# Routing products in shared turns of a PSUM bank, and a Gelu call ahead of its wait, in a two-layer attention and expert kernel

## The chip, the cores and the metric

The kernel runs on one core of one Trainium2 chip. The metric is the device time of one execution in microseconds (us). TensorE is called PE below, VectorE DVE, ScalarE ACT, GpSimd POOL, and SyncE, which here only issues DMAs, SP.

## The reference, cut to what matters

The input is 32 items of 256 tokens, 128 wide. Two layers of attention, each followed by the same expert layer, are added to the running value x:

```python
x = x + attention_a(layernorm(x))     # 16 heads of 8, biases, two masked scores
x = x + ffn(layernorm(x))
x = x + attention_b(layernorm(x))     # 16 heads of 8, no biases
x = x + ffn(layernorm(x))

def ffn(x):                            # per item
    pooled = x.mean(axis=1)
    gate = softmax(pooled @ gate_w.T)              # 8 experts
    top_w, top_i = top_k(gate, 2)
    top_w = top_w / (top_w.sum(-1, keepdims=True) + 1e-08)
    h = gelu(einsum('bsd,bkcd->bksc', x, down_w[top_i]) + down_b[top_i])
    h = h * top_w
    return einsum('bksc,bkdc->bsd', h, up_w[top_i]) + (top_w * up_b[top_i]).sum(1)
```

So each item must be through its attention before its two experts are known, and the choice of experts is a short chain of very small operations: a product with gate_w, top 2 of 8, a softmax, and then the weights and biases of the chosen experts.

## The kernel before, in words

**Turns and steps.** There are 64 turns: turn t is item t of layer 1 for t below 32, item t-32 of layer 2 above. A written-out software pipeline of steps n = -6 to 70 runs all of them; each step has eight sub-steps p = 0 to 7, one for each pair of heads, and each engine's program is a function `step(engine, n, p)` called in that order. In one step the engines work on several turns: the layer norm of turn n+5, projections of q and k of turn n+4 (L890), v of turn n+3 (L918), the scores whose row maximum is sought of turn n+2 (`max_side`, L786, read by DVE's reduction L597), the transposed maxima of turn n+1 (L878), the scores that are exponentiated, of turn n (`exp_side`, L800, read by ACT's L669), and their products with v (`weigh`, L771); the end of the attention of turn n-1 (L902, L617, L929, L736 or L738, L954), the addition to x of turn n-2 (L587), and the second norm of turn n-3 (L941, L746, which also gives the pooled value).

**PSUM.** Three pairs of banks form a ring for scores, exponentials and expert products; `uses` (L288 and after) lists in which order they take it, and `fill_pair` waits for the reader of three uses before. One bank, `values_bank`, is for `weigh`. One bank, `m_bank`, is the side bank: all other products take it in turns. Before each turn PE calls `fill_m` (L153), which waits until the reader of the turn before is through.

**Bursts.** The expert layer is done for groups of four turns, group g in step BURSTS[g] (L223). In a burst PE does `down` (L812) at p = 4, ACT does four Gelu calls (L705) at the end of p = 3, PE does `up` (L827 and L835) at p = 5, and DVE adds to x (L632). Exp and Gelu lie in different tables of ACT, and a table load stands ahead of the first Gelu and of the next Exp. POOL copies the chosen experts' weights ahead of the burst (`prepare`, L420, at p = 3: one turn a step in the four steps before the burst for turns below 40, then two a step); the last eight turns' up weights are made by DVE at p = 4 (L648).

**Batches.** The experts are chosen for batches of 8, later 4 turns (L221). `batch_at(n, after)` (L239) says which batch has its moment in step n. Before the change the moments of a batch (first turn f, r rows) are:

- step f+r+3: at p = 4 PE's `logits` (L848) takes a turn of the side bank, DVE's `best_of` (L544 to L550, five linked operations) reads it at p = 4, ACT's exponential (L753) is at p = 6;
- step f+r+4: DVE's `weights_of` (L560 to L564) at p = 0, ahead of the addition L587, and `spread` (L572 to L576) at p = 2; PE's `mixes` (L854, L857) takes a turn of the side bank at p = 4, between L902 and L918, and ACT copies its results (L712, L713) at p = 3; SP sends the indices (L389) to where POOL can load them;
- step f+r+5: PE's `biases` (L864, L865) takes a turn at p = 4, ACT copies (L720, L721), POOL splits the bias in three (`split_biases`, L442) at p = 7.

DVE's operations on a batch are linked: each waits for the semaphore of the one before (`link`, L520).

## Time and profile before

| what | value |
|---|---|
| time, median of 3 runs | 1024.27 us (1018.36 to 1024.57) |
| the profiled execution's own time | 1024.45 us |
| its span, in which all rows below lie | 1022.6 us |
| first step with work of all kinds (n = 0) begins | 52.51 us |
| step 62 begins | 963.11 us |

The profiled execution took 1.85 us more than its span, and 0.2 us more than the median of the runs.

Steps are told apart in the trace by L412, POOL's first operation of p = 0, of which there is one in each step: the start of step n is taken as the start of the L412 for turn n+1. A window from one to the next is one step.

### The profile page before, as it was taken

The numbers are of one execution on the slowest core, as the hardware profiler recorded it, in microseconds if no ns is written. First come the engines' busy times: TensorE is split into PE (matmuls) and PEld (weight loads), VectorE is DVE, ScalarE is ACT, GpSimd is POOL, SyncE is SP. The second block draws the span as 40 slices with busy tenths as digits, with TensorE's granted clock in tenths as the row PEclk, the third lists the DMA queues.
The fourth block names the chain that finished last, engine by engine and source line by source line (L and its number), as shares of the span: only waits on it lengthen the run. The fifth ranks groups of instructions, "written<-read, shape, count | busy, mean of one in ns | idle before, by whom it ended". The sixth has DMA issues, their size and how long they took to land.

```text
span 1022.6 us, 27845 instructions
## 1 busy us (share of the span) xinstructions
PE 928.4 (91%) x10286; PEld 515.9 (50%) x10286; DVE 787.7 (77%) x1394; ACT 767.8 (75%) x1280; POOL 666.7 (65%) x1280
## 2 busy tenths in 40 slices
PE   2589999989999899989999999998999899998985
PEld 1245555545554555545555455555555455555444
DVE  1778888878878788787878878786887868877624
ACT  2168888868887788877887778876888778787863
POOL 8455666648767767575767667676675758773532
PEclk9889999989999999999999999998999999999987
DMA  6576455444434445343454435444354535445001
GB/s 186 152 225 196 142 139 174 134 118 137 146 113 138 130 109 148 114 146 87 136 146 129 121 105 153 117 139 122 100 149 135 150 85 162 124 117 151 12 22 42
DMA packets 144695, 131.68 MB, mean 129 GB/s; under 512 B 9616, under 2 KB 127536, under 8 KB 144432
## 3 DMA queue, kind: packets, MB, share of 16 engines
q1 hardware_dynamic: 143456, 128.49, 43.7%
q8 instruction: 83, 1.36, 0.6%
q10 hardware_dynamic: 1104, 1.41, 0.5%
q14 instruction: 52, 0.43, 0.1%
HBM read 73.76 MB, written 55.57 MB: 126 GB/s over the span
## 4 chain that ended last, share of the span: by engine, by line
PE 71%; ACT 9%; DVE 8%; issue 7%; DMA 2%; POOL 2%; ACTq 1%; SPq 0%; DVEq 0%; POOLq 0%
PE values_bank L771 22%; PE ring L786 12%; PE ring L800 11%; PE m_bank L890 6%; DVE nmax L597 6%; PE m_bank L918 4%; PE m_bank L954 3%; PE m_bank L941 3%; PE m_bank L902 3%; PE m_bank L929 2%; ACT probs L669 2%; ACT hT L705 2%; DMA k_stack<-scratch 2%; PE ring L835 1%; ACT qk L689 1%
## 5 line engine op out<-in xcount | busy, mean ns | idle before, releaser
L597 DVE TENSOR_REDUCE nmax<-ring 128x4 f32<-128x1024 f32 x512 | 605.7, 1220 | 127.1 <-PE ring L786 126.4
L669 ACT ACTIVATE probs<-ring 128x1024 f32<-128x1024 f32 x512 | 517.8, 1026 | 48.1 <-PE ring L800 43.6
L771 PE MATMUL values_bank<-probs,values 128*32 128x256 f32 x4096 | 277.5, 389 | 1.3 <-ACT probs L669 1.2
L786 PE MATMUL ring<-k_stack,q_stack 64*128 64x256 bf16 x2048 | 202.5, 278 | 24.3 <-DMA k_stack<-scratch 18.7
L488 POOL TENSOR_SCALAR xy<-x,mv,rstd 128x128 f32<-128x128 f32 x256 | 200.7, 794 | 7.9
L800 PE MATMUL ring<-q_stack,k_stack 64*128 64x256 bf16 x2048 | 190.8, 276 | 0.7 <-DVE nmax L597 0.2
L412 POOL TENSOR_SCALAR mparts<-nmax 128x32 bf16<-128x32 f32 x64 | 13.9, 217 | 226.4 <-DVE nmax L597 226.4
L771 PEld LDWEIGHTS values_bank<-probs,values 128*32 128x32 f32 x4096 | 107.6, 110 | 92.6 <-issue 39.5
L786 PEld LDWEIGHTS ring<-k_stack,q_stack 64*128 64x128 bf16 x2048 | 70.1, 95 | 136.7 <-issue 61.0
L800 PEld LDWEIGHTS ring<-q_stack,k_stack 64*128 64x128 bf16 x2048 | 79.0, 95 | 84.6 <-issue 48.0
L504 POOL TENSOR_TENSOR rest<-qk,parts 128x512 f32<-128x512 f32 x64 | 74.0, 1157 | 5.4
L510 POOL TENSOR_TENSOR parts<-rest,parts 128x512 bf16<-128x512 f32 x64 | 74.0, 1156 | 5.4
L481 POOL TENSOR_TENSOR rstd<-varp,minus_half 128x4 f32<-128x4 f32 (+1 forms) x72 | 69.4, 964 | 6.0
L730 ACT COPY values<-m_bank 128x128 f32<-128x128 f32 x128 | 29.0, 280 | 57.1 <-PE m_bank L918 57.1
L528 DVE BATCH_NORM_STATS2 raw<-x 128x6 f32<-128x128 f32 x256 | 60.9, 280 | 11.1 <-DMA x<-in_x 11.1
L587 DVE TENSOR_TENSOR x<-x,m_bank 128x256 f32<-128x256 f32 x64 | 27.0, 422 | 46.8 <-PE m_bank L954 46.5
L941 PE MATMUL m_bank<-ident,xy 128*128 128x128 f32 x256 | 45.6, 297 | 13.0 <-ACT wb L192 9.0
L501 POOL TENSOR_SCALAR parts<-qk 128x512 bf16<-128x512 f32 x64 | 39.5, 618 | 19.6 <-ACT qk L690 18.6
L743 ACT COPY xnT<-m_bank 128x256 f32<-128x256 f32 x64 | 23.8, 372 | 37.1 <-PE m_bank L941 36.9
L680 ACT COPY oT<-values_bank 128x512 f32<-128x512 f32 x64 | 37.4, 585 | 18.2 <-PE values_bank L771 18.2
L902 PE MATMUL m_bank<-ident,oT 128*128 128x128 f32 x256 | 41.9, 286 | 2.7 <-ACT oT L680 0.8
L507 POOL TENSOR_SCALAR parts<-rest 128x512 bf16<-128x512 f32 x64 | 39.5, 618 | 5.9
(100 smaller groups left out, 1083.3 us busy)
## 6 DMA issues: line engine op xcount, KB each, us to landing
q_stack<-scratch SPq DMA_DIRECT2D x128, 256.0 KB
k_stack<-scratch SPq DMA_DIRECT2D x128, 256.0 KB
scratch<-parts SPq DMA_DIRECT2D x128, 192.0 KB, 2.1
scratch<-parts SPq DMA_DIRECT2D x128, 128.0 KB, 2.1
scratch<-parts SPq DMA_DIRECT2D x128, 64.0 KB, 2.4
out<-x SPq DMA_DIRECT2D x16, 256.0 KB, 2.7
x<-in_x SPq DMA_DIRECT2D x3, 768.0 KB, 6.6
q_stack<-maxT SPq DMA_DIRECT2D x128, 12.0 KB
```

The lines of the kernel that those rows point to most:

```text
L481: nc.gpsimd.tensor_tensor(rstd[i][:, both, :], varp[i][:, both, :], minus_half[:, both, :], ALU.pow).then_inc(rstd_done, 1)
L488: last = nc.gpsimd.tensor_scalar(xy[i][:, m, t, :], x[:, (turn % ITEMS) * TILES + t, :], mv[i][:, m, t, 0:1], rstd[i][:, m, t:t + 1], ALU. ...
L504: nc.gpsimd.tensor_tensor(rest[i][:, :, :], qk32[i][:, :, :], parts[i][:, 0], ALU.subtract).then_inc(rest_done, 1)
L510: nc.gpsimd.tensor_tensor(parts[i][:, 2], rest[i][:, :, :], parts[i][:, 1], ALU.subtract).then_inc(parts_ready, 1)
L597: nc.vector.tensor_reduce(dst, src, axis=AX.X, op=ALU.max, negate=True).then_inc(max_done, 1)
L669: nc.scalar.activation(probs[g % 2][:, c:c + 2, :, :], pair_of("exps", n, p)[:, :, :].rearrange("p x (k q) -> p x k q", k=TILES), ACT.Exp) ...
L771: last = nc.tensor.matmul(values_bank[32 * c:32 * (c + 1), a * TOKENS:(a + 1) * TOKENS], values[turn % RING][:, k, PER_GROUP * g + c, :], ...
L786: last = nc.tensor.matmul(pair_of("scores", turn, p)[:, a, t * TOKENS:(t + 1) * TOKENS], q_stack[z][rows, p, t * P:(t + 1) * P], k_stack[z ...
L800: last = nc.tensor.matmul(pair_of("exps", turn, p)[:, a, k * TOKENS:(k + 1) * TOKENS], k_stack[r][rows, p, k * P:(k + 1) * P], q_stack[r][ ...
L890: last = nc.tensor.matmul(m_bank[:, a * TOKENS:(a + 1) * TOKENS], wmat, xnT[(n + 4) % 2][:, :], start=(a == 0), stop=(a == 1), skip_group_ ...
L902: last = nc.tensor.transpose(m_bank[:, at:at + P], oT[(n - 1) % 2][:, a, t * P:(t + 1) * P], ident[:, :])
L941: last = nc.tensor.transpose(m_bank[:, at:at + P], xy[(n + 5) % 2][:, m, t, :], ident[:, :])
```

## The change

- `logits` now stands at p = 7 of step f+r+2, in the side bank's columns 256 to 263, in the turn of the output projection L954 that follows it in the same turn (columns 0 to 255); the next taker of the bank waits for `best_of`'s first reading.
- `best_of` stands at p = 0 of step f+r+3, behind the addition L587 and ahead of the step's first maximum; ACT's exponential is at p = 2; `weights_of` and `spread` are at p = 5, behind the additions of a burst.
- `mixes` stands at p = 1 of step f+r+4 in columns 128 to 287, and `biases` at p = 1 of step f+r+5 in columns 128 to 383, each sharing the turn of the transposed maxima L878, which as 16-bit values take the bytes of columns 0 to 127. ACT's copies stand behind its copy of the maxima (L676), ahead of `oT` (L680). `split_biases` stays in step f+r+5.
- BURSTS is new, so that for the batches of turns 8 to 47 step f+r+3 is a burst step. Its first eight entries are two steps later. The two-a-step preparation begins at turn 32 instead of 40.
- In a burst ACT calls Gelu on one column (`spare`) ahead of its first wait; in bursts of steps 64 and above it calls Exp on one column behind the last Gelu.
- DVE's up weights for turns 56 to 63 are made at p = 7 instead of p = 4.

```diff
-        BURSTS = (17, 21, 25, 29, 33, 37, 41, 45, 49, 53, 55, 57, 59, 63, 66, 70)
+        BURSTS = (19, 23, 27, 31, 35, 39, 43, 47, 49, 51, 54, 56, 58, 62, 66, 70)
...
-                early_step = burst - (1 if turn >= LATE else GROUP - j if turn < 40 else 2 - j // 2)
+                early_step = burst - (1 if turn >= LATE else GROUP - j if turn < ITEMS else 2 - j // 2)
...
-            return next((b for b, (first, rows) in enumerate(BATCHES) if first + rows + BACK + after == n), None)
+            return next((b for b, (first, rows) in enumerate(BATCHES) if first + rows + BACK - 1 + after == n), None)
...
-                    if p == 7 and batch_at(n, 2) is not None:
-                        split_biases(batch_at(n, 2))
+                    if p == 7 and batch_at(n, 3) is not None:
+                        split_biases(batch_at(n, 3))
...
-                    link(nc.vector.tensor_scalar(logit[rows, :], m_bank[rows, 0:EXPERTS], 1.0 / TOKENS, None, ALU.mult))
+                    link(nc.vector.tensor_scalar(logit[rows, :], m_bank[rows, TOKENS:TOKENS + EXPERTS], 1.0 / TOKENS, None, ALU.mult))
...
-                    if p == 0 and batch_at(n, 1) is not None:
-                        weights_of(batch_at(n, 1))
                     if p == 0 and live(n - 2):
...
+                    if p == 0 and batch_at(n, 1) is not None:
+                        best_of(batch_at(n, 1))
...
-                    if p == 2 and batch_at(n, 1) is not None:
-                        spread(batch_at(n, 1))
...
-                    if p == 4 and batch_at(n, 0) is not None:
-                        best_of(batch_at(n, 0))
...
+                    if p == 5 and batch_at(n, 1) is not None:
+                        weights_of(batch_at(n, 1))
+                        spread(batch_at(n, 1))
...
-                    if p == 4:
+                    if p == 7:
                         for turn in PREPARED.get(n, ()):
                             if turn >= FIRST_BY_VECTOR:
...
+                    if p == 0 and batch_at(n, 2) is not None:
+
+                        b = batch_at(n, 2)
+                        act.wait_ge(mixed_done, b + 1)
+                        if before_batch(b):
+                            act.wait_ge(wu_ready, before_batch(b))
+                        nc.scalar.copy(weight[b % 2][:, :], m_bank[:, WIDTH:WIDTH + ITEMS])
+                        nc.scalar.copy(hotT[:, :, :].rearrange("p a b -> p (a b)"), m_bank[0:TOP * EXPERTS, WIDTH + ITEMS:WIDTH + 5 * ITEMS]).then_inc(weight_ready, 1)
+                    if p == 0 and batch_at(n, 3) is not None:
+
+                        b = batch_at(n, 3)
+                        act.wait_ge(biases_done, b + 1)
+                        if b > 0:
+                            act.wait_ge(split_done, SPLITS * b)
+                        nc.scalar.copy(biasd[b % 2][:, :], m_bank[:, WIDTH:WIDTH + ITEMS])
+                        nc.scalar.copy(biasu[:, :], m_bank[0:3 * ITEMS, TOKENS:TOKENS + WIDTH]).then_inc(biases_ready, 1)
...
                         group = group_at(n)
+                        nc.scalar.activation(spare[:, group:group + 1], bqs[:, :], ACT.Gelu)
                         act.wait_ge(biases_ready, batch_of(group * GROUP) + 1)
...
+                        if n >= TURNS:
+                            nc.scalar.activation(spare[:, len(BURSTS) + group:len(BURSTS) + group + 1], bqs[:, :], ACT.Exp)
...
-                    if p == 6 and batch_at(n, 0) is not None:
-
-                        b = batch_at(n, 0)
+                    if p == 2 and batch_at(n, 1) is not None:
+
+                        b = batch_at(n, 1)
...
+                    if p == 1 and batch_at(n, 2) is not None:
+                        mixes(batch_at(n, 2))
+                    if p == 1 and batch_at(n, 3) is not None:
+                        biases(batch_at(n, 3))
                     if p == 1 and live(n + 1):
-                        fill_m(pe, maxT_ready, (n + 1) + 1)
+                        if batch_at(n, 2) is None and batch_at(n, 3) is None:
+                            fill_m(pe, maxT_ready, (n + 1) + 1)
...
-                    if p == 4 and batch_at(n, 0) is not None:
-                        logits(batch_at(n, 0))
-                    if p == 4 and batch_at(n, 1) is not None:
-                        mixes(batch_at(n, 1))
-                    if p == 4 and batch_at(n, 2) is not None:
-                        biases(batch_at(n, 2))
...
+                    if p == PAIRS - 1 and batch_at(n, 0) is not None:
+                        logits(batch_at(n, 0))
                     if p == PAIRS - 1 and live(n - 1):
                         wo = projections[(n - 1) // ITEMS][3]
-                        fill_m(pe, x_ready, (n - 1) + 1)
+                        if batch_at(n, 0) is None:
+                            fill_m(pe, x_ready, (n - 1) + 1)
```

## Rows read from the trace of the kernel before

**Rows 1.** The page: busy time by engine, and shares of the chain that ended last.

```profile
PE 928.4 (91%) x10286; PEld 515.9 (50%) x10286; DVE 787.7 (77%) x1394; ACT 767.8 (75%) x1280; POOL 666.7 (65%) x1280
...
PE 71%; ACT 9%; DVE 8%; issue 7%; DMA 2%; POOL 2%; ACTq 1%; SPq 0%; DVEq 0%; POOLq 0%
```

**Rows 2.** Busy time in single steps 25, 31, 33, 35, 36, 13.

```profile
core 0: us, PE busy (x) PEld busy (x) DVE busy (x) ACT busy (x) POOL busy (x), PEclk, DMA share, GB/s
388.06:401.04 12.98, 12.88 (x153) 6.86 (x154) 11.48 (x19) 10.89 (x19) 10.10 (x20) 1.00 0.51 145
482.01:494.82 12.81, 12.78 (x153) 6.83 (x153) 11.48 (x19) 10.72 (x18) 10.11 (x20) 1.00 0.47 136
520.48:538.48 18.00, 16.78 (x181) 10.53 (x182) 12.95 (x21) 14.88 (x24) 10.10 (x19) 1.00 0.43 116
551.32:565.60 14.28, 13.00 (x155) 6.94 (x156) 12.16 (x24) 10.87 (x20) 10.10 (x19) 1.00 0.51 141
565.60:581.72 16.12, 14.77 (x158) 7.31 (x159) 13.00 (x27) 10.99 (x20) 10.16 (x19) 0.89 0.40 117
...
229.48:243.59 14.11, 13.57 (x157) 7.34 (x158) 11.57 (x19) 11.26 (x21) 11.79 (x24) 1.00 0.50 135
```

**Rows 3.** The same, summed over the three-step stretches of batches 0 to 7.

```profile
sum 392.69, PE 358.64 PEld 200.78 DVE 304.32 ACT 296.18 POOL 245.16; mean PE 44.83 PEld 25.10 DVE 38.04 ACT 37.02 POOL 30.65
```

**Rows 4.** Timeline of burst steps 33 and 63: start, us, engine, instruction, [idle before].

```profile
525.45 1.94 ACT L669 ACTIVATE probs<-ring 128x1024 f32<-128x1024 f32 x2
...
527.41 1.99 PE L812 MATMUL ring<-normT,wd 128*128 128x256 f32 x8
...
528.61 1.28 ACT L705 ACT_TABLE_LOAD   x1 [1.22 <-issue]
...
531.53 0.39 PE L827 MATMUL ring<-biasu_parts,pick 96*128 96x256 bf16 x2 [1.14 <-ACT hT L705]
...
978.70 1.28 ACT L705 ACT_TABLE_LOAD   x1 [0.42 <-issue]
```

**Rows 5.** Timeline of batch 3's steps 35 and 36, the product and linked operations.

```profile
559.50 0.14 DVE L544 TENSOR_SCALAR logit<-m_bank 8x8 f32<-8x8 f32 x1
...
559.70 0.71 PE L918 MATMUL m_bank<-wb,xnT 128*128 128x128 f32 x4 [1.25 <-DVE logit L544]
...
560.13 0.14 DVE L550 TENSOR_SCALAR nbest<-best 8x1 f32<-8x1 f32 x1
...
576.79 1.93 PE L771 MATMUL values_bank<-probs,values 128*32 128x256 f32 x16
```

**Rows 6.** Timeline of the last batch: first and last of weights_of and spread.

```profile
1007.92 0.20 DVE L560 TENSOR_SCALAR tsum<-e 4x1 f32<-4x1 f32 x1 [0.65 <-ACT e L753]
...
1009.41 0.17 DVE L576 TENSOR_TENSOR mix<-hot,wt 4x16 f32<-4x16 f32 x1
```

**Rows 7.** Timeline of the beginning of step 37.

```profile
582.30 0.42 DVE L587 TENSOR_TENSOR x<-x,m_bank 128x256 f32<-128x256 f32 x1 [0.73 <-PE m_bank L954]
...
582.70 3.49 DVE L597 TENSOR_REDUCE nmax<-ring 128x4 f32<-128x1024 f32 x3
...
584.28 0.39 PE L800 MATMUL ring<-q_stack,k_stack 64*128 64x256 bf16 x4
```

**Rows 8.** Timeline of POOL at the end of step 54, and splitting of batch 3's bias.

```profile
852.58 1.16 POOL L510 TENSOR_TENSOR parts<-rest,parts 128x512 bf16<-128x512 f32 x1
853.74 0.22 POOL L412 TENSOR_SCALAR mparts<-nmax 128x32 bf16<-128x32 f32 x1
...
593.02 0.29 POOL L448 TENSOR_SCALAR biasu_parts<-biasu 96x128 bf16<-96x128 f32 x1
...
594.64 0.42 POOL L456 TENSOR_TENSOR biasu_parts<-biasu_rest,biasu_mid 32x128 bf16<-32x128 f32 x1
```

**Rows 9.** Timeline of the end: steps 65 and 70.

```profile
998.85 2.54 DVE L648 TENSOR_SCALAR wu<-up_sb,weight 64x128 f32 x8 [2.89 <-issue]
...
1016.90 1.16 PE L835 MATMUL ring<-wu,hT 128*128 128x128 f32 x8 [0.34 <-ACT hT L705]
```

More of the change, by code:

```diff
@@ L120, in build @@
         biasd = [sb(f"biasd{i}", [P, ITEMS]) for i in range(2)]
+        spare = sb("spare", [P, 32])
         biasu = sb("biasu", [3 * ITEMS, WIDTH])
@@ L847, in logits @@
                         pe.wait_ge(consts_in, 16 * CONSTANTS)
-                    nc.tensor.matmul(m_bank[0:rows, 0:EXPERTS], pooled[:, at], gate_sb[:, :], start=True, stop=True).then_inc(logits_done, 1)
+                    nc.tensor.matmul(m_bank[0:rows, TOKENS:TOKENS + EXPERTS], pooled[:, at], gate_sb[:, :], start=True, stop=True).then_inc(logits_done, 1)
                 def mixes(b):
@@ L853, in mixes @@
                     pe.wait_ge(mixing, MIXING * (b + 1))
-                    nc.tensor.transpose(m_bank[:, 0:ITEMS], wide[:, :, :].rearrange("p a b -> p (a b)"), ident[0:ITEMS, 0:ITEMS])
+                    nc.tensor.transpose(m_bank[:, WIDTH:WIDTH + ITEMS], wide[:, :, :].rearrange("p a b -> p (a b)"), ident[0:ITEMS, 0:ITEMS])
                     for k in range(4):
                         src = (hot if k == 0 else mix)[:, :, :].rearrange("p a b -> p (a b)")
-                        last = nc.tensor.transpose(m_bank[0:TOP * EXPERTS, (k + 1) * ITEMS:(k + 2) * ITEMS], src, ident[0:ITEMS, 0:ITEMS])
+                        last = nc.tensor.transpose(m_bank[0:TOP * EXPERTS, WIDTH + (k + 1) * ITEMS:WIDTH + (k + 2) * ITEMS], src, ident[0:ITEMS, 0:ITEMS])
                     last.then_inc(mixed_done, 1)
@@ L863, in biases @@
                     pe.wait_ge(weight_ready, b + 1)
-                    nc.tensor.matmul(m_bank[:, 0:ITEMS], downb_sb[:, :], hotT[:, 0, :], start=True, stop=True)
-                    nc.tensor.matmul(m_bank[0:3 * ITEMS, WIDTH:2 * WIDTH], hotT[:, 1:4, :].rearrange("p a b -> p (a b)"), upb_sb[:, :],
+                    nc.tensor.matmul(m_bank[:, WIDTH:WIDTH + ITEMS], downb_sb[:, :], hotT[:, 0, :], start=True, stop=True)
+                    nc.tensor.matmul(m_bank[0:3 * ITEMS, TOKENS:TOKENS + WIDTH], hotT[:, 1:4, :].rearrange("p a b -> p (a b)"), upb_sb[:, :],
                                      start=True, stop=True).then_inc(biases_done, 1)
```

14 lines of the change are left out of this document (removed).

## The prediction

> **What bounds the kernel now.** I read the page's busy shares and its chain first. PE is busy 91% of the span and holds 71% of the chain that ended last; DVE, ACT and POOL are busy 77, 75 and 65% [rows 1]. So whatever makes PE idle costs time, and whatever the others do beside it costs nothing until it makes PE wait. Then I cut the run into steps. A plain step is 12.98 us in layer 1 and 12.81 in layer 2 with PE busy 12.88 and 12.78: PE is the whole step. DVE is busy 11.48 of it, ACT 10.9, POOL 10.1 [rows 2]. These give what each could take on for nothing: DVE 1.33, ACT 1.9 to 2.1, POOL 2.7 before its gaps between instructions.
>
> Everything above the plain step is what the change can touch. A burst alone makes a step 18.00, 5.19 more, of which PE works 4.00 (16.78 less 12.78) and idles 1.19. The first step of a batch is 14.28, the second 16.12, and the third 14.11 where no burst shares it, 1.47, 3.31 and 1.13 more, for 0.22, about 0.5 and 0.7 of PE's work [rows 2]. (In the second PE is busy 1.99 more at a granted clock of 0.89. Its products with v took 1.93, nearly twice the 1.07 of a plain step's, behind its waits: PE ran part of this step at 1.2 instead of 2.4 GHz [rows 2, 5].) The cause of the first is plain: `logits` has a turn of the side bank, and PE's next product waits 1.25 for DVE's reading, which stood behind DVE's long reductions [rows 5].
>
> **Gelu's table ahead of the wait.** In step 33 ACT's exponentials end at 527.39, it idles 1.22, loads the table from 528.61 (1.28) and then does four Gelu, and PE waits 1.14 for them before it may begin `up` [rows 4]. The idle time is the wait for the first two products of `down`. The new call lets the load begin at 527.4: table there at 528.7, the one-column Gelu about 0.2 more, so the first real Gelu starts at 528.9 instead of 529.9. The other two wait for the last `down` product at 529.40 and are not held by it. `up` may begin 1.0 earlier, inside the 1.14 that PE waits. So 1.0 a burst is gone; it is PE's time, as PE has work behind it. Thirteen bursts begin before step 62 in either order: 13.0. Bounds: 0.5 if the next Exp and its load become late instead, 1.19 (PE's whole idle time) at best: 6.5 to 15.5.
>
> One rule speaks against this. The Trainium skill (ScalarE: Activation LUTs, What ACT_TABLE_LOAD costs) says that a switch costs a drain of about 1.38 us beside the load of 1.283. If the idle 1.22 were that drain, the load could not come earlier and the gain would be nil. The load is 1.28 here too; but the idle time ahead of it is 1.22 in step 33 and 0.42 in step 63 [rows 4], as a wait for products would have it and a fixed drain not. By the rule the sum below would be 1002.7 instead of 989.0; it is rival 4.
>
> **The batches before.** The stretches of three steps of batches 0 to 7 sum to 392.69 [rows 3]. Without batches they would be 7 steps of 12.97, 15 of 12.82, steps 60 and 61 (where q, k and v of later turns are missing) of about 11.4 each, an estimate, and 8 bursts of 5.19: 90.8 + 192.3 + 22.8 + 41.5 = 347.4. The batches cost 45.3, 5.7 each.
>
> **The batches after.**
> - `logits`: its product is 0.22 of PE [rows 2] and has no wait of its own: the output projection L954 behind it uses the same turn, and L878 in the next step waits for DVE's first linked operation, 0.18 behind the addition it waited for anyway. 0.25.
> - `best_of`, now ahead of the step's first reduction: from 559.50 to 560.27, 0.8 us [rows 5], all five operations and gaps. DVE runs three reductions back to back from 582.70; PE's exponential-side product of p = 1 needs the first, done at 583.92, and started at 584.28 [rows 7]. So 0.36 is slack and 0.45 shows; the third reduction (3.49 for three) is tighter, and I take 0.7. Bounds 0.2 to 0.8. Behind it queue all of the step's maxima.
> - ACT's exponential of 0.3 to 0.5 between the third and fourth: 0.2, in front of Gelu.
> - `weights_of` and `spread`: from 1007.92 to 1009.58, 1.7 us [rows 6], at p = 5. Before, DVE's burst steps had 18.00 less 12.95 idle, 5 us [rows 2]; the operations fill the wait ahead of the reductions of p = 6, and PE needs these only a product with v later. 0.1 in a burst, 0.7 where there is none (batches 0, 6, 7), since a plain step leaves DVE 1.33. Bounds 0 to 1.7.
> - `mixes`: 0.5 of PE in p = 1, no wait for `o` ahead and none for ACT's copies behind, because L878 shares the turn and the copies fit into the time in which ACT waits for `weigh` before `oT`. 0.5.
> - `biases`: 0.7 in the same way.
> That is 2.45 for batches 1 to 5 and about 3.0 for 0, 6 and 7: 12.2 + 9.0 = 21.2. The gain is 45.3 less 21.2, 24.1. The least is PE's work alone, 1.45 a batch, 11.6 in all.
>
> **POOL and the queues.** In steps 52, 53 and 56, 57 POOL prepares two turns a step. A step with two preparations fills POOL wholly already: in step 54 it went from L510 (852.58 + 1.16) straight into the next step's L412 [rows 8]. Steps 53 and 57 have now no burst, and the split of the bias comes on top: 593.02 to 595.06, 2.0 [rows 8], less the 0.7 by which `biases` lengthens them. Behind it on POOL stand the split maxima, for which PE's L878 waits with nearly no slack. 1.4 twice: 2.8 lost. Bounds 0 to 5.6. The queue of SP gains nothing and loses nothing: the index DMA goes out a step ahead of its use, as before. The changed turns of the bursts let no later user of x or of the ring wait: each group is added to x before the item's second visit, seven steps ahead in the case of group 0.
>
> **The end.** From step 62 on, ACT's exponentials bind more than PE, and at the very end it is one chain. Gelu early: 0.4 in the burst of step 62 (its idle time of 0.42 [rows 4]) and 0.34 in the last, what `up` waited for Gelu [rows 9]. `mixes` out of the way of step 64's chain: about 0.4. In step 65 DVE's up weights (2.89 of register loads and waiting, 2.54 of work [rows 9]) move behind the statistics of the last turn, so these come 5 earlier; but the norm's transposes stand behind `up` in PE's queue, and `up` waits for these weights, now 0.8 later. I take 0 for it, bounds 2.5 won to 1.5 lost. Sum 1.2.
>
> **The sum.** 1024.45 - 13.0 - 24.1 + 2.8 - 1.2 = 989.0, against the profiled execution's own time; it stood 0.2 above the median, which I leave out. Check: from 52.5 to 963.1 PE cannot go below the sum of its work, and the kernel would need 910.6 - 34.3 = 876 there, still above 62 plain steps and 13 bursts of 4.0 (about 852) and the batches' own 12.
>
> **Rivals.**
> 1. The forecast, 989: chance 0.60.
> 2. All but PE's own work hides: batches cost 11.6, no loss on POOL, and the bursts as forecast. For it: ACT and DVE have 2 and 1.3 us to spare. Against: DVE's three reductions back to back. 1024.45 - 13.0 - 33.7 - 1.2 = 976.6. Chance 0.14.
> 3. DVE becomes the bound of each batch: `best_of` and `weights_of` with `spread` show in full, 0.8 + 1.7 beside 1.45 and 0.2 of ACT, 4.15 a batch, 33.2 in all; and Gelu gives only 0.5 a burst. 1024.45 - 6.5 - 12.1 + 2.8 - 1.2 = 1007.5. Chance 0.15.
> 4. The early Gelu does nothing, because what stands ahead of the table load is not the wait that it passes: 989.0 + 13.0 + 0.7 = 1002.7. For it: the trace names no releaser for that idle time, only "issue". Against: it varies. Chance 0.08. This is what the Trainium skill's drain (ScalarE: Activation LUTs, What ACT_TABLE_LOAD costs) would do.
> 5. Slower: PE's clock. The one batch step that stalls most in the kernel before has a granted clock of 0.89 for a stall of about 1.3; if the stall at the head of `best_of`'s step and what follows leaves PE at 1.2 GHz for most of the batch's three steps, 38 us of PE's work grow by up to a factor of two. At a granted clock of 0.75 that is 38.4 / 0.75 - 38.4 = 12.8 a batch on top of 2.65, for eight batches 124 against 45.3: 1024.45 - 13.0 + 78.5 + 2.8 - 1.2 = 1091. It decides from where a batch costs over 7.1 (45.3 and the net 11.4 of the other terms, by eight). Against it: 1.14 of idle in a burst left the clock at 1.00 [rows 2, 4]. Chance 0.03.
>
> **Numbers.** A measurement of this kernel tells about 1% from no change. Faster by over 1% (below 1014) holds in cases 1 to 4 but for their edges: 0.95; within 1% 0.03; slower 0.02. The range takes in rival 2 and reaches to rival 4: 976 to 1005.
>
> **What would show it.** Burst steps of about 17.0 with ACT's table load right behind the exponentials and no wait of 1.1 at L827; steps 34 (logits) at 13.1, 36 (mixes) at 13.3, 37 (biases) at 13.5, 35 (burst, `best_of`) near 18.0 with PE waiting for L597 at its start; steps 53 and 57 ending with POOL late and a PE wait for L418; steps before 10 unchanged. Wrong it would be if the load keeps its idle time ahead (rival 4), if step 35 is above 19 (rival 3), or if the granted clock falls below 0.95 in the batches' steps (rival 5).

## The result and the profile after

The changed kernel takes 991.04 us, the median of 4 runs (988.27 to 991.77), against 1024.42 (1018.36 to 1024.73) for the kernel before beside it: a ratio of 0.9692, with a 95% interval of 0.9657 to 0.9727. The forecast was 989.0 in a range of 976 to 1005. The profiled execution took 990.56 us; its span is 987.4, where the forecast less the 1.85 around the span of before was 987.15.

The page's busy shares and its chain, to be set beside [rows 1]:

```profile
PE 917.8 (93%) x10286; PEld 513.9 (52%) x10286; DVE 787.2 (80%) x1394; ACT 772.6 (78%) x1299; POOL 666.2 (67%) x1280
...
PE 67%; ACT 10%; DVE 9%; POOL 5%; issue 4%; DMA 3%; SPq 1%; POOLq 1%; ACTq 1%; DVEq 0%
```

The same products run, and yet PE is busy 10.6 us less, in a span 35.2 shorter. "Issue" fell from 7% of the chain to 4%: it is 7% again in e1 and 4% in e2 below, which differ from their base in the early Gelu call alone, so what left it is the wait ahead of Gelu's table. Next the busy time of single steps of the kernel after, cut as in [rows 2]: 34 (logits at its end), 35 (burst with `best_of`), 36 (mixes), 37 (biases), 47 (burst alone), then 53 to 57, and the whole stretch from step 0 to step 62:

```profile
core 0: us, PE busy (x) PEld busy (x) DVE busy (x) ACT busy (x) POOL busy (x), PEclk, DMA share, GB/s
514.58:527.42 12.84, 12.81 (x155) 6.83 (x155) 11.47 (x19) 10.66 (x18) 10.11 (x20) 1.00 0.49 149
527.42:545.60 18.18, 17.52 (x187) 11.01 (x188) 14.81 (x34) 15.88 (x27) 10.09 (x19) 1.00 0.36 111
545.60:558.33 12.73, 12.61 (x154) 6.65 (x155) 11.57 (x19) 10.36 (x20) 10.10 (x20) 1.00 0.42 135
558.33:571.80 13.47, 13.44 (x157) 7.34 (x158) 11.58 (x19) 11.04 (x20) 11.82 (x25) 1.00 0.53 153
697.46:714.36 16.90, 16.78 (x181) 10.53 (x182) 12.86 (x21) 14.98 (x25) 11.40 (x25) 1.00 0.39 121
787.91:802.82 14.91, 14.73 (x172) 7.99 (x171) 12.56 (x21) 12.26 (x21) 13.10 (x31) 1.00 0.64 190
802.82:821.16 18.34, 16.94 (x167) 10.31 (x167) 12.08 (x20) 13.80 (x24) 11.39 (x24) 0.91 0.34 104
821.16:837.27 16.11, 13.81 (x164) 7.49 (x164) 14.79 (x33) 11.77 (x20) 11.41 (x25) 1.00 0.41 126
837.27:854.05 16.78, 16.39 (x182) 10.15 (x177) 12.79 (x21) 14.58 (x27) 11.39 (x24) 1.00 0.45 135
854.05:868.95 14.90, 14.82 (x172) 8.08 (x172) 12.48 (x21) 12.25 (x21) 13.09 (x29) 1.00 0.38 114
...
52.79:926.28 873.49, 853.02 (x9825) 474.63 (x9826) 744.74 (x1280) 727.29 (x1206) 614.08 (x1168) 1.00 0.47 138
```

The same stretch of the kernel before:

```profile
52.51:963.11 910.60, 865.36 (x9825) 478.23 (x9826) 745.68 (x1280) 724.71 (x1193) 611.92 (x1159) 0.98 0.46 133
```

The reader is to see three things. A burst step went from 18.00 [rows 2] to 16.90, with PE busy 16.78 in both: its idle time went from 1.22 to 0.12. The batch's burst (35) costs 1.28 more than a burst alone, its second step (36) nothing, its third (37) 0.64. And the stretch to step 62 is 37.1 us shorter; 24.8 of that is idle time (45.2 before, 20.5 after) and 12.3 is PE's busy time with the granted clock at 1.00 instead of 0.98. About 2.2 of the 37.1 lie in step 0, ahead of every changed instruction: it took 14.73 before and 12.54 after, where PE waits for a DMA into `k_stack`, and between 13.2 and 15.7 in the experiments. So the part of the changed steps is 34.9, of which 24.0 is PE's idle time and 11.0 its busy time (1.3 of the 12.3 lie in step 0). In the profile of before, steps 12, 28, 36, 44, 45 and 52 have a granted clock below 1.00; in that of after step 54 alone has.

What became of the wait for Gelu's table, in the timeline of step 35 (start, duration; compare [rows 4]):

```profile
534.07 1.00 ACT L669 ACTIVATE probs<-ring 128x1024 f32<-128x1024 f32 x1
...
535.09 1.28 ACT L713 ACT_TABLE_LOAD   x1
...
536.38 0.20 ACT L713 ACTIVATE spare<-bqs 128x1 f32<-128x1 f32 x1
536.49 1.55 ACT L722 ACTIVATE hT<-ring,biasd 128x256 f32<-128x256 f32 x4
...
538.10 0.39 PE L830 MATMUL ring<-biasu_parts,pick 96*128 96x256 bf16 x2
```

The exponential ends at 535.07 and the load starts at 535.09. The first product of `up` (L830, L827 before) waits for nothing. The idle time ahead of this load is 0.02 in all thirteen bursts up to step 61; in the kernel before it was 0.93 to 1.35 there. The load for the next Exp had 0.02 to 0.56 ahead of it already before the change.

What `best_of` at the head of the step does, same timeline, some 5 us earlier:

```profile
528.77 0.11 PEld L886 LDWEIGHTS m_bank<-identb,mparts 128*128 128x128 bf16 x2 [0.21 <-DVE logit L545]
...
529.27 3.49 DVE L598 TENSOR_REDUCE nmax<-ring 128x4 f32<-128x1024 f32 x3
...
530.55 0.39 PE L803 MATMUL ring<-q_stack,k_stack 64*128 64x256 bf16 x4 [0.49 <-DVE nmax L598]
```

The transposed maxima (L886) are held by DVE's first reading for a moment only. Three reductions stand back to back as in [rows 7], but start later, and PE waits 0.49 for the first. The forecast had 0.45 for this.

### The profile page after: what moved, and what is told of

Read it like the earlier page. It is cut to its first block, busy times and chain, and to the rows that moved or that the text cites. A ratio compares the mean times of both kernels' runs of the same rounds, so it can differ in the third digit from the quotient of the medians.

```text
span 987.4 us, 27821 instructions
## 1 busy us (share of the span) xinstructions
PE 917.8 (93%) x10286; PEld 513.9 (52%) x10286; DVE 787.2 (80%) x1394; ACT 772.6 (78%) x1299; POOL 666.2 (67%) x1280
## 4 chain that ended last, share of the span: by engine, by line
PE 67%; ACT 10%; DVE 9%; POOL 5%; issue 4%; DMA 3%; SPq 1%; POOLq 1%; ACTq 1%; DVEq 0%
PE values_bank L774 21%; PE ring L789 11%; PE ring L803 10%; PE m_bank L898 6%; DVE nmax L598 5%; PE m_bank L910 4%; PE m_bank L959 3%; PE m_bank L943 3%; PE m_bank L920 3%; ACT probs L669 2%; PE m_bank L931 2%; ACT hT L722 2%; ACT L713 2%; DMA k_stack<-scratch 2%; DMA scratch<-parts 1%
## 5 line engine op out<-in xcount | busy, mean ns | idle before, releaser
L774 PE MATMUL values_bank<-probs,values 128*32 128x256 f32 x4096 | 274.9, 386 | 0.7 <-ACT probs L669 0.6
L774 PEld LDWEIGHTS values_bank<-probs,values 128*32 128x32 f32 x4096 | 107.1, 109 | 89.8 <-issue 37.2
L511 POOL TENSOR_TENSOR parts<-rest,parts 128x512 bf16<-128x512 f32 x64 | 74.1, 1158 | 5.4
L529 DVE BATCH_NORM_STATS2 raw<-x 128x6 f32<-128x128 f32 x256 | 60.9, 280 | 10.8 <-DMA x<-in_x 10.7
L586 DVE TENSOR_TENSOR x<-x,m_bank 128x256 f32<-128x256 f32 x64 | 27.0, 421 | 49.9 <-PE m_bank L959 49.9
L943 PE MATMUL m_bank<-ident,xy 128*128 128x128 f32 x256 | 44.9, 294 | 12.3 <-ACT wb L193 9.0
```

The lines of the kernel that those rows point to most:

```text
L511: nc.gpsimd.tensor_tensor(parts[i][:, 2], rest[i][:, :, :], parts[i][:, 1], ALU.subtract).then_inc(parts_ready, 1)
L529: last = nc.vector.bn_stats(raw[i][:, t, :], x[:, (turn % ITEMS) * TILES + t, :])
L774: last = nc.tensor.matmul(values_bank[32 * c:32 * (c + 1), a * TOKENS:(a + 1) * TOKENS], values[turn % RING][:, k, PER_GROUP * g + c, :], ...
L943: last = nc.tensor.transpose(m_bank[:, at:at + P], xy[(n + 5) % 2][:, m, t, :], ident[:, :])
```

## The experiments

e1 to e4 ran on one chip beside seven runs of the kernel before (median 1020.41 us), e5 to e8 on another beside one (1026.22), and e9 to e12 there beside eleven (1021.65). Step lengths are windows as above, from one profiled execution each. "Step 1 to 62" is the stretch from the start of step 1 to that of step 62; it leaves out step 0, which varies.

**1 and 2. Gelu's table.** e1 takes the early call out of the kernel after:

```diff
-                        nc.scalar.activation(spare[:, group:group + 1], bqs[:, :], ACT.Gelu)
```

> The changed kernel without the one-column Gelu call ahead of the wait. Theory: the call lets the table load overlap the wait for the first products of down, so without it a burst step without batch work (step 47) goes from 16.90 back to about 18.0, TensorE waits 1.1 at L830 again, and the kernel takes about 13 x 1.1 + 0.7 = 15 us more than 991: 1006 (ratio to the kernel before about 0.982). Rival (the drain or another stall ahead of the load is fixed, and the bursts got shorter by their new places): step 47 stays at 16.9 and the time within 2 us of 991.

e2 puts that line, and `spare`, into the kernel before and changes nothing else:

```diff
                         group = group_at(n)
+                        nc.scalar.activation(spare[:, group:group + 1], bqs[:, :], ACT.Gelu)
                         act.wait_ge(biases_ready, batch_of(group * GROUP) + 1)
```

> The kernel before with nothing but the one-column Gelu call. Theory: the gain of the call does not hang on the other edits: step 33 goes from 18.00 to 16.9, in all 1024.3 - 15 = 1009 (ratio about 0.985). Rival: in bursts that share a step with biases (steps 21, 29, 37, 45, 53, 57) the wait for the side bank, not Gelu, ends last, and half of the bursts give nothing: 1024.3 - 8 = 1016 (ratio 0.992).

Measured: e1 1005.26 us, ratio to before 0.984 (0.9791 to 0.9889); e2 1004.64, ratio 0.983 (0.9781 to 0.988). A burst alone in layer 2 is 18.00 in e1, as before, and 16.89 or 16.90 in e2, as after. The timeline of a burst in e1 (step 35):

```profile
540.01 1.00 ACT L669 ACTIVATE probs<-ring 128x1024 f32<-128x1024 f32 x1
...
542.18 1.28 ACT L721 ACT_TABLE_LOAD   x1 [1.18 <-issue]
...
545.10 0.39 PE L829 MATMUL ring<-biasu_parts,pick 96*128 96x256 bf16 x2 [1.14 <-ACT hT L721]
```

and in e2 (step 33, old place of everything else):

```profile
516.75 1.94 ACT L670 ACTIVATE probs<-ring 128x1024 f32<-128x1024 f32 x2
...
518.70 1.28 ACT L698 ACT_TABLE_LOAD   x1
...
521.71 0.39 PE L829 MATMUL ring<-biasu_parts,pick 96*128 96x256 bf16 x2
```

So the call is worth about 1.1 in most bursts in either surrounding, and rival 4 is out: without the call the load idles 1.18 behind the exponential, with it 0.01. The rival of e2's expectation is out too: a burst that shares its step with `biases` gains as much (29: 19.31 to 18.20). Less is gained where PE waited less for Gelu or still does: 0.69 in steps 55 and 59 of e2 (a wait of 0.49 before), 0.83 in step 39, where the kernel after still waits 0.30 for it. For thirteen bursts the steps of e2 give 13.8. From step 1 to step 62, e1 needs 14.2 us more than the kernel after. In e2 the same stretch is 21.1 shorter than before, 7.3 more than 13.8; experiment 12 shows what that remainder is. By the medians e2 is 15.8 under the kernel before beside it.

**3. The burst schedule.** e3 keeps everything but gives the bursts and the preparation their old steps:

```diff
-        BURSTS = (19, 23, 27, 31, 35, 39, 43, 47, 49, 51, 54, 56, 58, 62, 66, 70)
+        BURSTS = (17, 21, 25, 29, 33, 37, 41, 45, 49, 53, 55, 57, 59, 63, 66, 70)
...
-                early_step = burst - (1 if turn >= LATE else GROUP - j if turn < ITEMS else 2 - j // 2)
+                early_step = burst - (1 if turn >= LATE else GROUP - j if turn < 40 else 2 - j // 2)
```

> The changed kernel with the burst steps and the preparation rule of before, so that for batches 1 to 5 the vector operations stand in plain steps and the biases in burst steps. Theory (a plain step has 1.3 us of VectorE to spare and takes a batch's operations for about 0.6 more than a burst step does; POOL's overflow in steps 53 and 57 goes): steps 35 and 43 about 12.82 + 1.9 = 14.7, steps 53 and 57 without a POOL wait; 5 x 0.6 = 3 lost and 4 won back: 990, the same as the changed kernel. Rival (a plain step cannot take them, as step 55 of the changed kernel suggests, 3.2 above plain with its follower): steps 35 and 43 near 16, 5 x 1.9 = 9.5 lost, 4 won: 996.

Measured: 987.99 (987.71 to 988.25), ratio 0.9667 (0.9621 to 0.9713): not slower than the kernel after, whose ratio is 0.9692. The steps show why. The first line is a plain step with all of `best_of`, `weights_of` and `spread` (35), the second the third step of that batch, here a burst:

```profile
534.83:550.12 15.29, 13.79 (x163) 7.47 (x164) 13.98 (x33) 11.75 (x20) 10.10 (x19) 1.00 0.45 132
...
562.85:580.37 17.52, 17.41 (x185) 11.01 (x186) 12.96 (x21) 15.36 (x27) 11.78 (x24) 1.00 0.39 117
```

In a plain step DVE's batch operations cost 15.29 less 12.83, 2.46, between the theory's 1.9 and the rival's 3.2; in a burst 18.18 less 16.90, 1.28. So standing in bursts is worth about 1.2 a batch in layer 2 (1.0 in steps 19 and 27), and from step 1 to step 49 the kernel after is indeed 3.9 ahead of e3. From step 49 to 62 it loses 6.0: its steps 53 and 57 overflow on POOL, batches 6 and 7 still have `best_of` in plain steps (55 and 59), and a drop of the clock (below) is 1.5 of it. The new schedule as a whole is not a gain; the batches' new places are. Up to step 62, e3 differs from e2 only in these places and in the shared turns: 858.9 us from step 1 to 62 against 874.8, 15.9 less. In e2 3.3 of this lie in its steps 52 and 56, where the granted clock is 0.90 and 0.89.

Step 55 of the kernel after costs more than e3's plain step, 16.11. Its timeline:

```profile
832.82 1.16 POOL L511 TENSOR_TENSOR parts<-rest,parts 128x512 bf16<-128x512 f32 x1
...
832.98 1.08 DVE L574 COPY wide<-wt 4x128 f32<-4x128 f32 x1
...
836.03 0.39 PE L803 MATMUL ring<-q_stack,k_stack 64*128 64x256 bf16 x4 [1.76 <-DVE nmax L598]
```

The copy of `spread` takes 1.08 here, beside POOL's L511, and 0.21 in the steps of the other batches; in e3's step 35 PE's wait at this place is 0.96. So 0.8 of step 55 is the slow copy. It is there in all eight profiles with this schedule and not in e3, e8 and e10. That POOL's operation holds it is likely from the times, and was not tested.

**4. The shared turns.** e4 leaves `mixes` and `biases` at p = 1 but gives them a turn of the side bank of their own, with ACT's copies ahead of the maxima's:

```diff
-                        if batch_at(n, 2) is None and batch_at(n, 3) is None:
-                            fill_m(pe, maxT_ready, (n + 1) + 1)
+                        fill_m(pe, maxT_ready, (n + 1) + 1)
...
```

ACT's copy L676 moves behind L684 to L693.

> The changed kernel in which mixes and biases take a turn of the side bank of their own at p = 1, ahead of that of the transposed maxima (ScalarE copies their results first). Theory (sharing the turn is worth what TensorE would wait for two ScalarE copies): 0.5 to 0.9 us a step in two steps of each of eight batches, 8 x 2 x 0.7 = 11: 1002, and some clock below 1.00 in these steps. Rival (TensorE has work of values ahead that hides the copies, the place at p = 1 alone was the gain): within 3 us of 991.

Measured: 998.78 (996.07 to 1000.33), ratio 0.9767 (0.9717 to 0.9817). Step 36 is 0.68 longer than the 12.73 after, with the same work of PE:

```profile
550.52:563.93 13.41, 12.61 (x154) 6.64 (x155) 11.58 (x19) 10.44 (x20) 10.10 (x19) 1.00 0.46 140
```

and from its timeline:

```profile
552.44 0.29 PE L885 MATMUL m_bank<-identb,mparts 128*128 128x128 bf16 x2 [0.77 <-ACT hotT L679]
```

PE waits 0.77 for the copy of `hotT` before it may write the maxima. Step 37 is 14.01 instead of 13.47. Over all batches sharing is worth 8.2 us (step 1 to 62: 867.7 here, 859.45 in the second profile of the kernel after), where 11 were expected. With turns of their own at p = 1, `mixes` and `biases` still cost 0.58 and 1.18 over a plain step. In the kernel before, at p = 4, steps 36 and 37 cost 1.84 (with DVE's weights, 14.67 in e2) and 1.31 (18.20 in e2 less its burst's 16.89). The rest of the batches' gain lies in the places of DVE's and PE's operations together; they were not tested one by one.

**5. POOL's overflow.** e5 moves `split_biases` from p = 7 of the batch's third step to p = 0 of the next, behind the split maxima:

```diff
-                    if p == 7 and batch_at(n, 3) is not None:
-                        split_biases(batch_at(n, 3))
...
+                    if p == 0 and batch_at(n, 4) is not None:
+                        split_biases(batch_at(n, 4))
```

> The changed kernel with POOL's split of the bias moved from the end of a batch's third step to behind the split maxima of the next. Theory (in steps 53 and 57 the two preparations and this split overfill POOL, and PE waits for L419 in the step behind): the wait of 1.46 ahead of L886 at the start of step 54 goes, with the fall of the granted clock behind it; steps 53 and 54 together from 33.25 to about 30.4 + 0.2, 57 and 58 from 31.76 to 30.4; the time about 4 lower, 987. Rival (POOL stays too full, and the norm's transposes or the split parts are late instead): 53 and 54 together stay above 32, or steps such as 22 and 30, plain until now, grow.

Measured in one run: 988.23. Step 53 is 13.34 instead of 14.91 and step 57 13.44 instead of 14.90, so the split is what made them late, 1.5 each. But the steps behind the third steps of batches 1 to 4 are 13.18 instead of 12.95 (layer 1) or 12.81, as the rival said, and step 56 is 19.45 instead of 16.78:

```profile
789.67:803.01 13.34, 13.31 (x157) 7.21 (x157) 11.57 (x19) 10.91 (x20) 11.42 (x25) 1.00 0.65 190
...
836.00:855.45 19.45, 19.28 (x182) 11.33 (x177) 12.98 (x21) 14.62 (x27) 11.39 (x24) 0.82 0.36 115
```

In the long one PE is busy 19.28 for the work of 16.39: it ran part of it at 1.2 GHz, behind the wait of 1.76 at the end of step 55. From step 1 to 62 the gain and these losses come to within 1 us of nothing, where 4 won were expected.

**6. The order of index and store at the end.** SP issues the last index DMA ahead of the two stores of group 14 in the kernel after. The stores are in step 67 in both kernels, a step behind burst 66; the index DMA has moved with the batches from step 68 to 67, and in SP's step its block stands ahead of that of the stores. e6 exchanges the two blocks in SP's step, so that the index DMA L390 comes behind this:

```diff
+                    group = group_at(n - 1) if n <= LAST else None
+                    if group is not None and group * GROUP >= ITEMS:
+                        store(sp, group)
...
-                    group = group_at(n - 1) if n <= LAST else None
-                    if group is not None and group * GROUP >= ITEMS:
-                        store(sp, group)
```

> The changed kernel with SyncE's store of a group ahead of the index DMA in the same step. Theory (the two stores of group 14, 512 KB, run just behind the last index DMA and slow POOL's first load of a register from 0.57 to 1.59 us, and down then begins 1 us later with PE's clock still low): from the index DMA to the first L429 4.2 us instead of 5.2, and the end 1 to 2 us earlier. Rival (the slow load has another cause, as the queue state or the position of the code): still 5.2, and no gain.

Measured in one run: 987.30. The chain that ended last, near the end, in the kernel after:

```profile
969.44 1.60 DMA index<-which
971.04 0.03 issue
971.07 1.59 POOLq L324
...
976.31 3.75 PE ring L815 x8
980.07 0.43 PE ring L830 x2
```

in the kernel before:

```profile
1007.12 1.64 DMA index<-which
...
1008.78 0.57 POOLq L323
```

and in e6:

```profile
971.03 0.57 POOLq L324
...
975.22 3.75 PE ring L815 x8
```

POOL's first load of an index into a register takes 1.59 in the kernel after and 0.57 in the other two. From the index DMA to `down` (L815, L812 before) it is 5.85 before, 6.87 after, 5.86 in e6, and 6.87 to 6.90 in the eight other profiles that have the stores behind the index, e3 with its old bursts among them. So 1.0 us of the end is this order, and it came with the batches' new places and not with the new bursts. From step 62 on e6 takes 58.5, against 61.1 after and 59.5 before; what it has won beyond 1.0 lies in the pieces that vary without the change (below).

**7. `best_of` split.** e7 leaves only the first of its five operations, the one that frees the side bank, at p = 0, and puts the other four at p = 2 behind the reductions, with ACT's exponential at p = 3:

```diff
                     link(nc.vector.tensor_scalar(logit[rows, :], m_bank[rows, TOKENS:TOKENS + EXPERTS], 1.0 / TOKENS, None, ALU.mult))
+
+                def rest_of_best(b):
...
+                    if p == 2 and batch_at(n, 1) is not None:
+                        rest_of_best(batch_at(n, 1))
...
```

> The changed kernel with only best_of's first operation ahead of the step's maxima and the other four at p = 2 behind the statistics, ScalarE's exponential at p = 3. Theory (0.8 us ahead of three back-to-back reductions is what makes PE wait 0.49 for L598 at the start and again before the third): step 35 from 18.18 to about 17.6, with L803 no longer waiting 0.49; eight batches, 4 to 5 us in all. Rival (the reduction at p = 3 is as tight, so the wait only moves): step 35 stays within 0.2 of 18.18.

Measured in one run: 983.84. Step 35 is 17.73 instead of 18.18, step 59 14.18 instead of 14.73:

```profile
527.25:544.98 17.73, 17.48 (x188) 11.03 (x188) 14.68 (x34) 15.79 (x27) 10.10 (x20) 1.00 0.41 115
```

and from its timeline:

```profile
528.48 3.49 DVE L602 TENSOR_REDUCE nmax<-ring 128x4 f32<-128x1024 f32 x3
...
532.27 0.14 DVE L550 MAX8 best<-logit 8x8 f32<-8x8 f32 x1
```

The reductions start 0.6 earlier against the step's start than in the kernel after, and the four small operations fit in behind. In six of the eight batches 0.5 of `best_of`'s cost was its place ahead of the reductions; from step 1 to 62 it makes 3.0 against the second profile of the kernel after, where 4 to 5 were expected. Step 55 stayed at 16.10, with the same wait of 1.76 near its end, and step 11 at 14.9.

**8. Another schedule.** e8 puts bursts also over the third steps of the small batches:

```diff
-        BURSTS = (19, 23, 27, 31, 35, 39, 43, 47, 49, 51, 54, 56, 58, 62, 66, 70)
+        BURSTS = (19, 23, 27, 31, 35, 39, 43, 47, 51, 53, 55, 57, 59, 62, 66, 70)
```

> The changed kernel with bursts 51, 53, 55, 57, 59 in place of 49, 51, 54, 56, 58, so that biases and their split (53, 57) and best_of (55, 59) fall on burst steps, at the price of a plain step 51 under batch 5's vector operations. Theory (stated from the step lengths of the changed kernel and of e3): 53, 57 near 17.5, 55 and 59 near 18.1, 51 near 15.3; steps 49 to 61 in all 195.9, as in e3, against 199.2, so step 62 begins about 3.3 earlier than in the changed kernel. Rival (each burst has its own cost that depends on the distance to the last one): no gain.

Measured in one run: 983.07. (The expectation named 51 a plain step; it is a burst, and 49 is plain. Its 195.9 for e3 is not what e3 took, 193.1.) Steps 49 to 61 took 192.04, where the kernel after needs 199.09, 7.0 less instead of the 3.3 expected:

```profile
726.88:918.92 192.04, 186.70 (x2134) 107.23 (x2135) 161.14 (x280) 161.13 (x268) 138.62 (x303) 1.00 0.42 128
```

PE's products are as many; 1.7 less busy time and 5.3 less idle. The lower clock in step 54 of after is 1.5 of the 7.0. All of the loss that e3 does not have is gone, with the early bursts kept.

**9. The up weights at the end.** e9 returns DVE's up weights of turns 56 to 63 to their old place:

```diff
-                    if p == 7:
+                    if p == 4:
                         for turn in PREPARED.get(n, ()):
                             if turn >= FIRST_BY_VECTOR:
```

> The changed kernel with VectorE's up weights for the last eight turns back at p = 4. Theory (what the earlier statistics win, up's later start loses): PE's wait of 0.98 for L648 ahead of L830 in step 66 goes, the last statistics come 5 us later, and from the last L586 (turn 63) to the index DMA it takes 11.6 as before the change, against 11.29: 0.3 lost. Rival (the move to p = 7 costs what up waits): 10.5, 0.8 won.

Measured in one run: 990.56. The wait of 0.98 for L648 is gone and the last statistics come later, as expected. From the last addition of attention (turn 63, L586) to the index DMA it is 11.86, against 11.29 and 11.42 in the two profiles of after and 11.58 and 11.59 in those of before. The move is worth about half a microsecond at most, in one run.

**10. All that helped.** e10 has the schedule of e8, the split of e7 and the order of e6.

> What helped, together: the bursts of e8, best_of split as in e7, the store ahead of the index as in e6. Theory (the three act on different steps and add): 991 less 7.0 (of which 1.4 is a clock episode that the changed kernel's profile has and others had not), 2.8 and 1.0, about 980 to 981, ratio to the kernel before about 0.957 to 0.96; steps 35 and 43 at 17.73, 53 and 57 at 17.4, 55 and 59 at about 17.7. Rival (they share the gain, as the same waits of TensorE): 983, like the best of them alone.

Measured: 978.12 (975.49 to 979.06, 6 runs) against 1021.65 (11 runs): ratio 0.9559 (0.9527 to 0.9591). It beats both kernels. From step 1 to 62 it needs 850.5 us, the kernel after 861.0 and 859.45; against the latter it wins 9.0, e8 alone 5.5 and e7 alone 3.0, so the two add, as the theory said. Step 53, burst, biases and two preparations at once, is the case in point: 17.48 where the kernel after has 14.91 without a burst.

```profile
781.54:799.02 17.48, 17.37 (x185) 10.96 (x185) 12.96 (x21) 15.31 (x27) 13.14 (x30) 1.00 0.56 164
```

Its end is no shorter: 60.9 from step 62 on. In e8 and e10, and in e4, the last addition of attention stands 12.9 to 13.5 before the index DMA instead of 11.3; why was not looked into.

**11 and 12. Both kernels profiled again**, unchanged.

> The changed kernel once more, unchanged, for a second profile. Theory (whether a stall also costs a fall of TensorE's clock depends on when it comes, not on the step): all steps repeat within 0.03 us but for those behind a stall of about 1.5 us, where step 54 is 16.85 or 18.34; the first step differs by up to 2 us. Rival (it belongs to the step in this kernel): step 54 is 18.34 again.

> The kernel before once more, unchanged. Theory: steps 12, 28, 36, 44, 45 and 52, where its profile has a granted clock below 1.00, lie at their length with a full clock (15.3, 14.7, 14.7, 14.7, 19.3, 15.0) in some cases, and steps 20 and 56, at 14.7 there, may lie near 16.2; the other steps repeat. Rival: the same steps have the low clock again.

Measured: 988.09 and 1024.4. In the second profile of the kernel after, all steps from 1 to 61 are within 0.02 of the first, but one. Step 54 begins in both with a wait for POOL; the first profile:

```profile
804.14 0.27 PE L886 MATMUL m_bank<-identb,mparts 128*128 128x128 bf16 x2 [1.46 <-POOL mparts L419]
...
804.34 1.94 PE L774 MATMUL values_bank<-probs,values 128*32 128x256 f32 x16
```

the second:

```profile
805.25 0.27 PE L886 MATMUL m_bank<-identb,mparts 128*128 128x128 bf16 x2 [1.46 <-POOL mparts L419]
...
805.45 1.07 PE L774 MATMUL values_bank<-probs,values 128*32 128x256 f32 x16
```

and that step as a window of the second profile:

```profile
803.92:820.78 16.86, 15.42 (x167) 9.72 (x167) 11.99 (x20) 13.77 (x24) 11.40 (x24) 1.00 0.41 113
```

The same wait of 1.46 is followed by products of 1.94 in the one and 1.07 in the other, and the step takes 18.34 or 16.86. In the kernel before, the same happens to a batch's second step. Step 28 in its first and its second profile:

```profile
446.58:462.71 16.13, 14.77 (x158) 7.41 (x159) 13.01 (x27) 11.08 (x20) 10.16 (x20) 0.89 0.42 118
```

```profile
447.76:462.43 14.67, 13.30 (x158) 6.99 (x159) 13.01 (x27) 11.08 (x20) 10.18 (x19) 1.00 0.47 129
```

Six steps of before (12, 20, 21, 28, 52, 53) differ by about 1.5 between its two profiles, in both directions. Steps 36, 44 and 45 have the lower clock in both and 56 in neither, as the rival said of them. So most batches of the kernel before have one or two places where PE's clock may fall, and in six of these steps it changes from execution to execution whether it does. Its runs say the same: the eleven beside e10 go from 1018.39 us at a mean granted clock of 0.978 to 1028.75 at 0.968. This is the remainder of e2: with the early call its step 36 is 14.67 at clock 1.00, where the two profiles of before have 16.12 and 16.31, steps 28, 36, 44 and (beside the call's 1.1) 45 are 1.5 and step 12 2.9 shorter than in the first profile of before, and step 56, with the lower clock here, is 1.5 longer, in all 7.2. Whether the early call itself makes the fall less likely is open. Between steps 1 and 61 the profiles of before have six and seven steps with the clock below 1.00 and e2 has two; the eleven profiles with the batches' new places have one or none.

It is the same for the wait of 1.76 at the end of step 55: in both profiles of after the granted clock behind it stayed at 1.00, and in e1 and e5 the next step has 0.91 and 0.82 (18.98 and 19.45 us). In e4, e6 and e7, which have this wait too, it stayed. Each fall in steps 1 to 61 of all profiles follows waits of 1.2 to 1.8 in sum, more than half of them in two pieces, as 0.91 and 0.42 in step 28 of before; none follows the 1.14 of a burst.

## Why the prediction was right, step by step

By spans, the forecast was 34.3 less to step 62 and 1.2 less behind it, 35.5 in all, 987.1. Measured: 34.9 less from the changed steps, 2.2 less in step 0, 0.3 later start, and 1.5 more at the end: 1022.64 - 34.9 - 2.2 + 0.3 + 1.5 = 987.4 (with rounding). The execution then took 3.2 around its span instead of 1.85.

- *Gelu's table ahead of the wait*: 1.0 a burst forecast, 1.10 in layer 2 and 1.20 in layer 1 measured, 13.8 by the single steps of e2 instead of 13.0. In a burst alone it became PE's whole idle time but for 0.12, near the upper bound named. The load was no sooner possible than the end of the exponentials, as forecast. The drain of about 1.38 us that the Trainium skill (ScalarE: Activation LUTs, What ACT_TABLE_LOAD costs) puts beside the load of 1.283 is not there: the load is 1.28, starts 0.02 behind the exponential, and the one-column call starts 0.01 behind the load.
- *The batches after*: 2.45 for batches 1 to 5 forecast; steps 35 to 37 less two plain ones (12.83) and a burst (16.90) come to 1.82, and 1.86 in layer 1. Logits, `best_of`, ACT's exponential and the weights together were forecast at 1.25 and show as 1.28 in step 35; biases at 0.7 and show as 0.64. `mixes` were forecast at 0.5 and do not show: step 36 is 12.73. The windows are cut at a POOL instruction, so a tenth or two may be shifted between neighbours, but the sum is 0.6 under the forecast. For a batch outside bursts e3 has 2.46 + 0.62 - 0.10 = 3.0, as forecast, but batch 6 cost 3.8 without POOL's part (steps 55 to 57: 47.79, less two plain steps, a burst and 1.45): the other 0.8 is the copy of 1.08 in step 55. Over all eight the batches' cost is 20.4 by the same count as the forecast's 21.2.
- *The batches before*: the 45.3 were right as a sum over that execution, but not a fixed price: 1.5 in each of several steps was the clock, and may be there or not. By the lengths of the same steps at a granted clock of 1.00 (in e2 or the second profile; step 45 by its like, 37) it was 10.5 of the 45.3. The forecast took step 36's clock for a property of its stall.
- *POOL*: 1.4 in each of steps 53 and 57 forecast (its own terms, 2.0 less 0.7, give 1.3); 1.44 and 1.43 measured (against 13.47), and 1.5 by e5. PE's wait is at L886 for L419, the last of the split maxima, at the head of step 54, as forecast: L418 is the same operation in the kernel before. POOL prepares two turns a step also in steps 47 to 50, 54 and 55, which the forecast did not list. What it left out is that a wait of this length may be followed by a lower clock: another 1.5 in step 54 of the profiled execution.
- *The end* is the step that failed, by 2.7 us: 1.2 won was forecast, 1.5 lost was measured (59.54 us from step 62 on before, 61.08 after; 59.55 and 60.39 in the second profiles). The forecast said "The queue of SP gains nothing and loses nothing: the index DMA goes out a step ahead of its use, as before", which was read from the middle of the kernel. In the last steps the index DMA has no step in hand, and moved to step 67 with its batch it stands ahead of the stores instead of behind: 1.0 lost (e6). Of the parts forecast 0.85 shows up to the index DMA: 0.56 up to the last addition of attention, 0.3 from there to the index DMA, where the up weights' move lies. Against them stand, beside the 1.0, 0.7 from `down` to the last addition to x, where PE at a granted clock of 0.50 took 3.75 for `down` instead of 3.38 and more for `up`, and 0.7 behind that addition. Those two vary between the kernels here, 6.8 to 7.9 and 2.7 to 3.7, without an order that the changes explain; the two profiles of one kernel (after) give 7.6 and 7.9. They stay unexplained.
- *The rivals*: 4 (no effect of the call) fell with e1 and e2. 3 (DVE binds) would have had step 35 above 19; it has 18.18. 2 (all hides) was right for `mixes` alone. 5 (the clock) had its mechanism, but the other way round: the stretch's clock rose from 0.98 to 1.00. That the change did this by taking stalls away fits the fewer falls in all eleven profiles with the new places; which stall counts is not shown.

What was right for a partly wrong reason: by step lengths 10.5 of the 34.9 us were clock won back, less 1.5 for step 54; with a granted clock of 1.00 in both, by this estimate, the changed steps would be 25.9 shorter (885.4 against 859.45). The forecast had the 10.5 inside the 45.3 of the batches, as if every stall of that kind always paid it. There is luck in the closeness: the 24 runs of the kernel before on record have a median of 1022.2 us, 2.2 under the profiled execution from which the sum was made, the 2.2 of step 0 were not forecast, and the end's error went the other way.

## What to carry to other kernels

Where the next function's table load stands behind a wait for data, a one-column call of that function ahead of the wait takes the load out of it; look for an idle time ahead of ACT_TABLE_LOAD that varies from place to place. Before small operations are moved into the steps with slack, count what the moved schedule does to every other engine's fullest steps, because here the gain of 1.0 to 1.2 a batch in four batches was given back in steps 53, 55, 57 and 59; and look at the very end on its own, where DMAs that have a step in hand elsewhere have none. A stall of 1.2 to 1.8 us on TensorE had two prices here, with and without the clock, so one profile of before shows one draw of them: profile it twice before a sum is built on it.

## What was not expected of the hardware

- The same stall of 1.46 us, in the same place of the same kernel, is followed by TensorE at 1.2 GHz in one execution and at 2.4 in another: the 16 products of L774 took 1.94 or 1.07, the step 18.34 or 16.86. Behind waits of 0.49 (step 35 of after), 0.77 (step 36 of e4) and 1.76 (step 55 of after) the clock stayed at 1.00, as behind 1.14 in [rows 2, 4]; behind the same 1.76 it fell in e1 and e5. No limit can be read from these.
- A register load by GpSimd from SBUF took 1.59 us behind two stores issued by SyncE at 970.09 and 970.58, and 0.57 where the stores had gone out before the index: 1.57 to 1.60 in nine profiles, 0.56 or 0.57 in the five with the other order. The loads that follow it take 0.15 in both kernels. That the stores' traffic is what holds it is the likely reading, since only their order was changed; the mechanism was not taken apart.
- A copy of 4x128 values by VectorE (`wide`, L574) took 1.08 us in step 55 of the kernel after and 0.21 in other steps of the same profile, and so again in the second profile.
